# A graph layer on one core: gathers begun in fours at given counts of tiles

## The chip, the cores and the metric

One NeuronCore of a Trainium2 chip runs the whole kernel. The metric is the device time of one execution in microseconds, the median of several runs. Five engines work side by side, each through its own queue in order: TensorE (PE in the profile; PEld is its weight load), VectorE (DVE), ScalarE (ACT), GpSimd (POOL) and SyncE (SP). They wait for one another by semaphores.

## The reference

A layer of a graph network with 12,500 nodes and 400,000 edges, 64 features, edges sorted by their destination:

```python
h = feat_src @ node_w.T
rf = review_feat @ review_w.T
m = (h[src_idx] + rf) * edge_w
x = _layernorm(x + segment_sum(m, dst_idx, num_segments=12500))
```

For each edge the row of its source node and the edge's own attributes are multiplied by two 64x64 matrices, added, weighted and summed into the row of the destination node; the result is added to x and normalized over the features.

## The kernel before

Both products are linear, so the kernel sums first and multiplies once at the end: `sums` holds, for each node, 64 weighted sums of source rows and 64 of edge attributes. Edges come in tiles of 128, and the tiles are worked in two ways that share the engines.

**Units.** The first 116 x 2048 edges form 116 units of 16 tiles. SyncE loads a unit's attributes (L410), GpSimd gathers the rows of x for each of its 16 tiles by an indirect DMA, 128 rows of 256 bytes (L490), into one of four slots of `rows`. TensorE then sums the unit (`sum_unit`, L1156, instructions on L1166) with 32 matmuls, waiting for the attributes, for all 16 gathers (L1161) and for the buffer. ScalarE copies the result, TensorE brings it into a window of 128 nodes (`multiply_unit`, L1177) and VectorE adds the window to `sums`. Sums of a unit raise `unit_summed`, which frees its slot: the gathers of unit u wait for the sums of unit u - 4 (L485). Four units make a batch, whose indices are prepared together (`src_ready`).

**Counted tiles.** The other 1269 tiles (`COUNTED`) need no gather. For each tile VectorE makes two one-hot matrices (`hot_key` L746, `hot_lo` L747), TensorE multiplies them into a table of counts (six matmuls, L1235, raising `counted` once a tile) and ScalarE copies the table out (L1048). They go in 71 groups: group 0 has `GT0` = 9 tiles, each other one `GT` = 18. After a group's tiles TensorE multiplies the table with the whole of x (`sum_x`, L1260, 196 instructions); half way through, it turns the next group's indices (L1212 to L1216) and sometimes a batch's (L1150 to L1153).

**The order of the work** is written out by hand, and the same on all engines. Groups 1 to 70 are steps of seven rounds of ten; a step takes `STEPS` = 2, 1, 2, 1, 2, 2, 1, 2, 1, 2 units along. The first unit of a step is summed ahead of the group's tiles, the second, if there is one, after six of them. So ten groups take 16 units and 180 tiles. Six rounds are a hardware loop, the last is written out. After the groups the last four units (112 to 115) are summed in the tail, behind the multiplication of most nodes' sums (L1289).

**GpSimd's queue** holds, after some constants, the gathers of all units in order, and at the end the scaling of some blocks of the output (L575). In the loop a unit's bounds of waits depend on the round, so they are computed in registers. `gathers_begun` is raised once a unit; nothing waits for it.

Of the kernel before, what the change touches and what calls it, by code (L numbers as in the profile page):

```python
# [43 lines left out]
GT = 18  # L44
HOT_BUFS = 3
SPAN = 7
UT = 16
SLOTS = 4
BATCH = 4
CYCLE = 16  # L50
UNITS = 116
STEPS = (2, 1, 2, 1, 2, 2, 1, 2, 1, 2)
LATE_UNITS = 4
PAD = 32
BEGUN = 2
FAR = -1000.0
LN_EPS = 1e-5
# [2 lines left out]
def build(nc, x, src, dst, attr, weight, node_w, review_w, out):  # L60
# [7 lines left out]
    COUNTED = (EDGES - COUNTED_FROM) // P  # L68
    GROUPS = (COUNTED - 1) // GT + 1
    GT0 = COUNTED - (GROUPS - 1) * GT  # L70
# [2 lines left out]
    HI = (NODES - 1) // P + 1  # L73
    HALF = HI * SPAN // 2
    ROUND_GROUPS = len(STEPS)
    ROUNDS = (GROUPS - 1) // ROUND_GROUPS - 1
    BT = BATCH * UT
    BATCHES = UNITS // BATCH
    QUADS = P // PAD
    BLOCKS_U = UT // QUADS  # L80

    assert EDGES == ALL_CHUNKS * CHUNK and 2 * F == P
    assert sum(STEPS) == CYCLE and CYCLE == 4 * BATCH and SLOTS == BATCH and UNITS % BATCH == 0
    assert GROUPS - 1 == (ROUNDS + 1) * ROUND_GROUPS and UNITS == (ROUNDS + 1) * CYCLE + LATE_UNITS
    assert GT0 >= HOT_BUFS and GT % HOT_BUFS == 0 and UNITS <= P and GROUPS <= P
# [22 lines left out]
    with ExitStack() as ctx:  # L108
        def sb(name, shape, dt=F32):
            return ctx.enter_context(nc.sbuf_tensor(name, shape, dt))  # L110
# [24 lines left out]
        slot_dst = sb("slot_dst", [P, BATCH, BATCH * BLOCKS_U])  # L135
        unit_hot = [sb(f"unit_hot{b}", [P, UT, PAD]) for b in range(2)]
        slot_hot = [sb(f"slot_hot{b}", [P, BLOCKS_U, WIN]) for b in range(2)]
# [44 lines left out]
        at, g_dst = part(0, GROUPS, [GT, P], I32)  # L182
        at, g_lo_hi = part(at, GROUPS, [2, GT])
        at, g_wide = part(at, GROUPS, [2, GT])
        at, g_bad = part(at, GROUPS, [1, 8])
        at, u_dst = part(at, UNITS, [UT, P], I32)
        at, u_lo_hi = part(at, UNITS, [2, UT])
        at, u_wide = part(at, UNITS, [2, UT])
        at, u_bad = part(at, UNITS, [1, 8])
        at, u_last = part(at, UNITS, [1, 1])  # L190
        at, slot_far = part(at, NS, [2, GT])
        at, bad_row = part(at, 1, [1, GROUPS + UNITS])
        at, u_rows = part(at, 1, [2, UNITS])
        at, g_worst = part(at, 1, [1, 2])
        at, calm = part(at, 1, [4, LATE_UNITS])
# [4 lines left out]
        at, dst_i = part(0, ALL_CHUNKS, [1, CHUNK], I32)  # L200
        at, ones = part(at, P, [1, P])
        at, lo_diag = part(at, ALL_CHUNKS, [1, ALL_CHUNKS])
        at, lo_hi_col = part(at, ALL_CHUNKS, [1, 2])
        at, lo_hi_row = part(at, 1, [2, ALL_CHUNKS])
        at, windows_i = part(at, 1, [2, ALL_CHUNKS], I32)
        at, windows_f = part(at, 1, [2, ALL_CHUNKS])
        at, lo_all = part(at, P, [1, ALL_CHUNKS])
        at, base_tab = part(at, 1, [1, ALL_CHUNKS], I32)
        at, window_tab = part(at, 1, [1, ALL_CHUNKS + 1], I32)
        at, src_sb = part(at, P, [CHUNK_SLOTS, TILES], I32)  # L210
        at, dst_sb = part(at, P, [CHUNK_SLOTS, TILES], I32)
        at, w_sb = part(at, P, [CHUNK_SLOTS, TILES])
        at, dst_left = part(at, P, [1, TILES])
        at, scatter = part(at, P, [PART_BUFS, PER_PART * WIN])
# [47 lines left out]
        gathers_begun = sem("gathers_begun")  # L262
# [30 lines left out]
        counted = sem("counted")  # L293
# [62 lines left out]
        def round_steps(r):  # L356

            i, adds = 0, r * (CYCLE + ROUND_GROUPS) + 1
            for n, size in enumerate(STEPS):
# [3 lines left out]
                if isinstance(r, int) and batch and batch.q >= BATCHES:  # L363
                    batch = None
                yield Step(r * ROUND_GROUPS + n + 1, units, batch, adds)
                i += size
                adds += size + 1

        last_units = [unit_at(ROUNDS + 1, i) for i in range(LATE_UNITS)]
        last_adds = (ROUNDS + 1) * (CYCLE + ROUND_GROUPS) + 1  # L370

        def each_unit(eng, do):

            with eng.Fori(0, ROUNDS + 1) as r:
                for i in range(CYCLE):
# [17 lines left out]
        def _(sp):  # L393
# [11 lines left out]
            def load_attr(unit):  # L405

                s = unit.i % SLOTS
                if not isinstance(unit.u, int) or unit.u >= SLOTS:
                    sp.wait_ge(unit_summed, unit.u - SLOTS + 1 + BEGUN)
                sp.dma_start(rows[:, s, :, F:2 * F],  # L410
# [38 lines left out]
            with sp.If(is_narrow(sp) == 1):  # L449
                for i in range(SLOTS, CYCLE):  # L450
                    load_unit(unit_at(0, i))
                with sp.Fori(1, ROUNDS + 1) as r:
                    for i in range(CYCLE):
# [23 lines left out]

        @block.gpsimd
        def _(pool):
            def gather_unit(unit):  # L480

                s, c = unit.i % SLOTS, unit.i // BATCH
                pool.wait_ge(src_ready, unit.b + 1)
                if not isinstance(unit.u, int) or unit.u >= SLOTS:
                    pool.wait_ge(unit_summed, unit.u - SLOTS + 1 + BEGUN)  # L485

                pool.sem_inc(gathers_begun, 1)
                for t in range(UT):
                    k = unit.i % BATCH * UT + t
                    pool.indirect_dma_start(  # L490
                        out=rows[:, s, t, 0:F], out_offset=None, in_=x,
                        in_offset=bass.IndirectOffsetOnAxis(ap=src_cols[:, c, k:k + 1].bitcast(U32), axis=0),
                    ).then_inc(gathered[s], 16)

            def gather_chunk(c, s, r):
# [5 lines left out]
                for k in range(TILES):  # L501
# [7 lines left out]
            pool.memset(first_mask[:, 1, :], 0.0).then_inc(masks_made, 1)  # L509
            pool.iota(quad_of[:, :], pattern=[[1, QUADS], [0, PAD]], base=0, channel_multiplier=0,  # L510
                      allow_small_or_imprecise_dtypes=True).then_inc(masks_made, 1)
# [67 lines left out]
        def _(dve):  # L579
# [27 lines left out]
            def make_unit_hot(unit):  # L607

                h, k = unit.i % 2, unit.i % BATCH * UT
                dve.wait_ge(batch_read, unit.b + 1)  # L610
                dve.wait_ge(unit_summed, unit.u - 1 + BEGUN)
                hot = unit_hot[h][:, :, 0:SPAN]
# [7 lines left out]
            def make_slot_hot(unit):  # L620

                k = unit.i % BATCH * BLOCKS_U
                dve.wait_ge(batch_read, unit.b + 1)
                dve.wait_ge(unit_multiplied, unit.u - 1 + BEGUN)
                dve.tensor_tensor(slot_hot[unit.i % 2][:, :, :],  # L625
# [4 lines left out]
            def copy_unit(unit):  # L630

                dve.wait_ge(unit_summed, unit.u + 1 + BEGUN)
                dve.tensor_copy(unit_slots[unit.i % 2][:, :], unit_ps[:, :]).then_inc(unit_copied, 1)

            def add_unit(unit, before):

                base = dve.value_load(unit_tab[0:1, bass.ds(unit.u, 1)], min_val=0, max_val=NODES - 1)
                dve.wait_ge(added, before)
                dve.wait_ge(unit_multiplied, unit.u + 1 + BEGUN)
                dve.tensor_tensor(sums[:, bass.ds(base, WIN)], sums[:, bass.ds(base, WIN)], unit_window_ps, ALU.add  # L640
# [192 lines left out]
            dve.memset(all_ones[:, :], 1.0)  # L833
            step(dve.tensor_scalar(part_i[:, 1:2], part_i[:, 0:1], PAD - 1, None, ALU.bitwise_and))
            step(dve.tensor_copy(part_f[:, 1:2], part_i[:, 1:2]))
# [306 lines left out]
        def _(pe):  # L1142
# [13 lines left out]
            def sum_unit(unit):  # L1156
# [6 lines left out]
                for b in range(BLOCKS_U):  # L1163
                    for j in range(QUADS):
                        t = b * QUADS + j
                        done = pe.matmul(unit_ps[j * PAD:(j + 1) * PAD, b * 2 * F:(b + 1) * 2 * F],  # L1166
                                         unit_hot[h][:, t, :], rows[:, s, t, :], start=True, stop=True)
# [223 lines left out]
```

## Time and profile before

| what | us |
|---|---|
| median of three timed runs | 2600.75 |
| lowest and highest of them | 2598.28, 2603.38 |
| span of the profiled execution | 4402.7 |
| TensorE matmuls busy in it | 2973.6 (68%) |
| VectorE | 1620.1 (37%) |
| ScalarE | 1200.5 (27%) |
| GpSimd | 1855.3 (42%) |

The profiled execution took 4402.7 us, and the shares are of that span; the timed runs are 1802 us shorter. All durations of single instructions below come from the profiled execution. In the rows of the trace an instruction stands with its start, its duration, its engine and its line; in square brackets is the idle time of its engine before it, and what ended it. "remote" is a semaphore whose rise came late or whose sender the trace doesn't tell. In the chain of waits every piece is what the end was waiting for at that time; "issue" there is time in which the engine waited for nothing that the profile shows.

### The profile page before, as it was taken

What the parts mean: (1) busy time and instruction counts of PE and PEld (TensorE: products, weight loads), DVE (VectorE), ACT (ScalarE), POOL (GpSimd) and SP (SyncE); (2) the same over time, 40 slices, a digit from 0 to 9 for tenths busy, and PEclk for the clock granted to TensorE, in tenths of its full rate; (3) what the DMA queues carried; (4) which work ended last, traced back from release to release, by engine and by line L of the source; (5) the groups of instructions that cost most, each with busy time, mean ns of one, the idle gap of its engine ahead of it and who ended that gap; (6) DMA issues with size and microseconds to landing.
All of it is one profiled execution on the core that took longest, in us unless ns stands there. A gap on an engine that the chain in (4) does not pass through costs nothing.

```text
span 4402.7 us, 74924 instructions
## 1 busy us (share of the span) xinstructions
PE 2973.6 (68%) x28844; PEld 2163.7 (49%) x28845; DVE 1620.1 (37%) x4276; ACT 1200.5 (27%) x1951; POOL 1855.3 (42%) x1885
## 2 busy tenths in 40 slices
PE   1767776776766766757777767777567567677676
PEld 1445553555544545535555545455345445455555
DVE  3333332343333333324333333333234333333334
ACT  0222222332222222213222222223223222222223
POOL 5444335434344443453344444443443344444342
PEclk9777787887777787778787777788778777777787
DMA  4121111111111121111111111211111122122111
GB/s 88 41 42 41 40 40 40 40 41 41 41 36 39 39 42 38 40 41 39 40 41 38 40 37 40 42 42 39 39 42 38 35 42 42 36 42 47 34 40 42
DMA packets 491784, 181.43 MB, mean 41 GB/s; under 512 B 449029, under 2 KB 461508, under 8 KB 491206
## 3 DMA queue, kind: packets, MB, share of 16 engines
q1 hardware_dynamic: 259490, 68.52, 7.2%
q0 software_dynamic: 59392, 60.94, 7.2%
q10 hardware_dynamic: 172510, 46.74, 4.9%
q8 instruction: 247, 4.05, 0.4%
q14 instruction: 145, 1.19, 0.1%
HBM read 172.85 MB, written 3.20 MB: 40 GB/s over the span
## 4 chain that ended last, share of the span: by engine, by line
PE 57%; another core or an unknown queue 27%; issue 10%; ACT 4%; DVE 1%; ACTq 1%; DVEq 0%; DMA 0%; SPq 0%; POOL 0%; POOLq 0%
PE count_ps L1235 30%; PE x_sums_ps L1260 18%; ACT counts L1048 4%; PE unit_ps L1166 3%; PE attr_ps L1227 2%; PE turn_ps L1177 1%; PE x_sums_ps L1268 1%; PE turn_ps L1215 1%; DVE hot_lo L747 0%; PE turn_ps L1212 0%; ACTq L1081 0%; PE x_sums_ps L1269 0%; PE attr_ps L1150 0%; DVE hot_key L746 0%
## 5 line engine op out<-in xcount | busy, mean ns | idle before, releaser
L490 POOL DMA_INDIRECT rows<-x,src_cols x1856 | 1845.6, 994 | 2475.0 <-PE unit_ps L1166 1434.0
L1235 PE MATMUL count_ps<-hot_key,hot_lo 128*128 128x343 bf16 x7614 | 1627.5, 366 | 1066.7 <-ACT counts L1048 613.5
L1235 PEld LDWEIGHTS count_ps<-hot_key,hot_lo 128*128 128x128 bf16 x7614 | 799.2, 115 | 1683.7 <-issue 842.1
L1048 ACT ACTIVATE counts<-count_ps 128x686 f32<-128x686 f32 x1269 | 1009.0, 803 | 1752.6 <-remote 947.4
L746 DVE TENSOR_SCALAR hot_key<-count,cols 128x686 bf16<-128x686 f16 x1269 | 531.5, 419 | 2128.6 <-remote 1185.3
L1260 PE MATMUL x_sums_ps<-counts,x_tab 128*64 128x126 f32 (+1 forms) x13916 | 804.6, 275 | 55.9 <-ACT counts L1048 54.8
L1260 PEld LDWEIGHTS x_sums_ps<-counts,x_tab 128*64 128x64 f32 x13916 | 771.2, 139 | 73.3 <-ACT counts L1048 68.8
L747 DVE SCALAR_TENSOR_TENSOR hot_lo<-count,cols 128x384 bf16<-128x384 f16 x1269 | 776.5, 612 | 0.0
L1166 PE MATMUL unit_ps<-rows,unit_hot 128*32 128x128 f32 x3712 | 223.1, 289 | 182.1 <-issue 176.2
L1227 PEld LDWEIGHTS attr_ps<-hot_rel,g_attr 128*128 128x128 f32 x1270 | 257.7, 230 | 94.9 <-issue 59.9
L1166 PEld LDWEIGHTS unit_ps<-rows,unit_hot 128*32 128x32 f32 x3712 | 123.3, 112 | 259.1 <-issue 252.5
L1227 PE MATMUL attr_ps<-hot_rel,g_attr 128*128 128x14 f32 x1270 | 222.2, 248 | 38.8 <-issue 31.1
L1021 ACT ACTIVATE unit_slots<-unit_ps 128x512 f32<-128x512 f32 x112 | 66.9, 598 | 530.6 <-remote 400.2
L1177 PE MATMUL turn_ps<-slot_hot,unit_slots 128*128 128x128 f32 x928 | 130.1, 286 | 0.6 <-DVE sums L640 0.6
L1177 PEld LDWEIGHTS turn_ps<-slot_hot,unit_slots 128*128 128x128 f32 x928 | 125.1, 203 | 7.9 <-issue 1.6
L1066 ACT ACTIVATE x_sums<-x_sums_ps 128x126 f32<-128x126 f32 (+1 forms) x71 | 19.6, 276 | 368.6 <-PE x_sums_ps L1260 368.6
L761 DVE TENSOR_TENSOR hot_rel<-column,cols 128x126 f32<-128x126 f32 (+1 forms) x71 | 20.6, 291 | 230.9 <-ACT cols L1032 230.9
L1030 ACT ACTIVATE slot_rel<-turn_ps,slot_no 126x1 f32<-126x1 f32 (+1 forms) x71 | 18.5, 261 | 318.4 <-PE turn_ps L1216 271.5
L782 DVE TENSOR_TENSOR sums<-sums,turn_ps 128x128 f32 x71 | 20.5, 289 | 199.1 <-PE turn_ps L1276 184.0
L625 DVE TENSOR_TENSOR slot_hot<-column,slot_dst 128x512 f32<-128x512 f32 x116 | 79.7, 687 | 2.6 <-issue 2.6
L605 DVE CAST src_cols<-attr_ps 128x64 int32<-128x64 f32 x29 | 6.5, 225 | 141.3 <-ACT rel_cols L1014 141.3
L1013 ACT ACTIVATE slot_dst<-attr_ps,part_f 128x16 f32<-128x16 f32 x29 | 7.9, 274 | 175.1 <-PE attr_ps L1153 175.1
(136 smaller groups left out, 953.1 us busy)
## 6 DMA issues: line engine op xcount, KB each, us to landing
rows<-edge_attr SPq DMA_DIRECT2D x116, 512.0 KB
g_attr<-edge_attr ACTq DMA_DIRECT2D x70, 576.0 KB, 4.6
rows<-x,src_cols POOLq DMA_INDIRECT x1856
out<-x_tab SPq DMA_DIRECT2D x10, 256.0 KB
g_idx<-src ACTq DMA_DIRECT2D x70, 9.0 KB
g_idx<-dst ACTq DMA_DIRECT2D x70, 9.0 KB
g_w<-edge_weight ACTq DMA_DIRECT2D x70, 9.0 KB
stage<-src SPq DMA_DIRECT2D x29, 32.0 KB
```

The lines of the kernel that those rows point to most:

```text
L490: pool.indirect_dma_start(out=rows[:, s, t, 0:F], out_offset=None, in_=x, in_offset=bass.IndirectOffsetOnAxis(ap=src_cols[:, c, k:k + 1].b ...
L625: dve.tensor_tensor(slot_hot[unit.i % 2][:, :, :], column[:, :].unsqueeze(1).to_broadcast([P, BLOCKS_U, WIN]), slot_dst[:, unit.i // BATCH ...
L746: dve.tensor_scalar(hot_key[h][:, :], count16[:, :], cols[:, KEY, t:t + 1], None, ALU.is_equal)
L747: made = dve.scalar_tensor_tensor(hot_lo[h][:, :, :], count16[:, 0:P].unsqueeze(1).to_broadcast([P, 3, P]), cols[:, LO, t:t + 1], cols[:, ...
L1021: act.activation(unit_slots[unit.i % 2][:, :], unit_ps[:, :], ACT.Copy).then_inc(unit_copied, 1)
L1048: act.activation(counts[:, :, t * SPAN:(t + 1) * SPAN].rearrange("p (a h) d -> p a h d", a=2), count_ps[t % 2][:, :, 0:HALF].rearrange("p ...
L1166: done = pe.matmul(unit_ps[j * PAD:(j + 1) * PAD, b * 2 * F:(b + 1) * 2 * F], unit_hot[h][:, t, :], rows[:, s, t, :], start=True, stop=True)
L1177: done = pe.matmul(unit_window_ps, unit_slots[unit.i % 2][:, b * 2 * F:(b + 1) * 2 * F], slot_hot[unit.i % 2][:, b, :], start=(b == 0), st ...
L1215: pe.transpose(turn_ps[:, q * GT:q * GT + nt], packed[0:nt, q, :], ident[0:nt, 0:nt])
L1227: pe.matmul(attr_ps[0:(until - t) * F, t * SPAN:until * SPAN], g_attr[:, t:until, :].rearrange("p t f -> p (t f)"), hot_rel[:, t:until, :] ...
L1235: last = pe.matmul(count_ps[b][:, a, 0:HALF], hot_lo[h][:, i, :], hot_key[h][:, a * HALF:(a + 1) * HALF], start=(i == 0), stop=(i == 2))
L1260: done = pe.matmul(x_sums_ps[half * F:(half + 1) * F, 0:ns], x_tab[:, hi, :], counts[:, hi, 0:ns], start=(hi < 2), stop=(hi >= HI - 2))
```

## The change

From unit 4 on, GpSimd waits ahead of each four of a unit's 16 gathers until TensorE has counted a given number of tiles, and then raises `gathers_begun` once more. 64 gathers of a batch are spread over `BATCH_TILES` = 10 x 18 x 4 / 16 = 45 tiles; the count is that of an even spread, less `LEAD` = 28 tiles. For the k-th gather of batch b it is 45 b + 9 + (45 k / 64, rounded down) - 28. Where it is known at build time it is cut to `COUNTED`. The waits of a unit ahead of its first gather stay.

```diff
@@ -52,6 +52,8 @@
 STEPS = (2, 1, 2, 1, 2, 2, 1, 2, 1, 2)
 LATE_UNITS = 4
 PAD = 32
+BURST = 4
+LEAD = 28
 BEGUN = 2
 FAR = -1000.0
 LN_EPS = 1e-5
@@ -73,6 +75,7 @@
     HI = (NODES - 1) // P + 1
     HALF = HI * SPAN // 2
     ROUND_GROUPS = len(STEPS)
+    BATCH_TILES = ROUND_GROUPS * GT * BATCH // CYCLE
     ROUNDS = (GROUPS - 1) // ROUND_GROUPS - 1
     BT = BATCH * UT
     BATCHES = UNITS // BATCH
@@ -477,6 +480,12 @@
 
         @block.gpsimd
         def _(pool):
+            def tiles_counted(unit, t):
+
+                at = GT0 + (unit.i % BATCH * UT + t) * BATCH_TILES // BT - LEAD
+                after = unit.b * BATCH_TILES + at
+                return min(after, COUNTED) if isinstance(after, int) else after
+
             def gather_unit(unit):
 
                 s, c = unit.i % SLOTS, unit.i // BATCH
@@ -486,6 +495,11 @@
 
                 pool.sem_inc(gathers_begun, 1)
                 for t in range(UT):
+                    if t % BURST == 0 and (not isinstance(unit.u, int) or unit.u >= SLOTS):
+                        after = tiles_counted(unit, t)
+                        if not isinstance(after, int) or after > 0:
+                            pool.wait_ge(counted, after)
+                            pool.sem_inc(gathers_begun, 1)
                     k = unit.i % BATCH * UT + t
                     pool.indirect_dma_start(
                         out=rows[:, s, t, 0:F], out_offset=None, in_=x,
```

## Rows read from the trace of the kernel before

**Rows 1.** The first line of the page of the kernel before.
```profile
span 4402.7 us, 74924 instructions
```

**Rows 2.** Three stretches, all engines: us, then busy us (instructions), granted clock, DMA share.
```profile
4341.94:4402.73 60.79, 35.72 (x362) 33.34 (x362) 33.21 (x75) 25.94 (x86) 5.87 (x7) 0.82 0.22 54
0.00:117.80 117.80, 27.79 (x301) 19.30 (x302) 46.44 (x123) 10.32 (x21) 65.03 (x86) 1.00 0.45 88
117.80:4341.94 4224.14, 2910.11 (x28181) 2111.11 (x28181) 1540.42 (x4079) 1164.29 (x1844) 1784.35 (x1792) 0.78 0.19 40
```

**Rows 3.** Who waited for whom, groups 1 to 70: us in total, times, longest.
```profile
POOL rows L490 <- PE unit_ps L1166: 1434.0, 64, 32.9
DVE hot_key L746 <- remote: 1161.7, 207, 23.8
```

**Rows 4.** Chain of waits without gathers: start us, us, what, instructions.
```profile
2038.26 0.13 PE attr_ps L1227 x2
...
2040.29 0.13 PE attr_ps L1227 x2
...
2042.35 0.81 ACT counts L1048
...
2043.21 5.59 PE x_sums_ps L1260 x98
...
2055.01 1.01 PE unit_ps L1166 x32
...
2056.60 0.18 PE attr_ps L1227 x2
```

**Rows 5.** Chain of waits around the group before, partly beside gathers.
```profile
1999.90 0.32 PE attr_ps L1150 x2
...
2000.67 0.30 PE turn_ps L1212 x2
...
2014.49 0.89 PE turn_ps L1177 x8
...
2019.59 4.43 issue
```

**Rows 6.** GpSimd in order of time: the first and the 64th gather.
```profile
9.82 1.15 POOL L490 DMA_INDIRECT rows<-x,src_cols  x1 [4.82 <-DVE src_cols L605]
...
89.29 0.95 POOL L490 DMA_INDIRECT rows<-x,src_cols  x1 [0.30 <-issue]
```

**Rows 7.** GpSimd, first and last of seven gathers beside counting.
```profile
2008.73 0.95 POOL L490 DMA_INDIRECT rows<-x,src_cols  x1 [29.32 <-PE unit_ps L1166]
...
2016.78 0.95 POOL L490 DMA_INDIRECT rows<-x,src_cols  x1 [0.30 <-issue]
```

**Rows 8.** GpSimd, last gather of unit 100 and first of unit 101.
```profile
3772.89 0.95 POOL L490 DMA_INDIRECT rows<-x,src_cols  x1 [0.30 <-issue]
3774.14 1.19 POOL L490 DMA_INDIRECT rows<-x,src_cols  x1 [0.30 <-issue]
```

**Rows 9.** TensorE in order of time: the unit's sums that free a slot.
```profile
2006.82 1.08 PE L1166 MATMUL unit_ps<-rows,unit_hot 128*32 128x128 f32 x32
```

**Rows 10.** All engines in order of time, the tail.
```profile
4328.84 13.06 PE L1260 MATMUL x_sums_ps<-counts,x_tab 128*64 128x126 f32 x196 [1.19 <-ACT counts L1048]
...
4368.28 1.05 POOL L575 TENSOR_TENSOR x_tab<-x_tab,counts 128x512 f32<-128x512 f32 x1 [42.70 <-DVE counts L822]
...
4373.30 13.22 ACT L1136 ACTIVATE x_tab<-x_tab,counts 128x64 f32<-128x64 f32 x55
...
4380.14 1.08 PE L1166 MATMUL unit_ps<-rows,unit_hot 128*32 128x128 f32 x32
```

**Rows 11.** Who waited for whom in the head, 50 to 117.8 us.
```profile
DVE hot_key L746 <- remote: 23.6, 2, 15.4
```

**Rows 12.** Two lines of the kernel: ns min/median/max, first and last start.
```profile
L490 POOL DMA_INDIRECT rows<-x,src_cols x1856: 942/947/1390, 9.8 to 4324.6; - x186
...
L485 POOLq ALU_OP  x84: 32/32/49, 614.7 to 4127.1; - x84
```

## The prediction

> **What bounds the kernel now.** The first thing to read is the distance between the two times: the profiled execution spans 4402.7 us [rows 1], the timed runs 2600.75 us. Nothing that is only said of the profiled execution may be sold as a gain, so I read the profile by stages to see which part of it the timed runs can contain.
>
> The stretches [rows 2] are the head up to the sums of group 0 (117.8 us), 70 groups (4224.1 us) and the tail (60.8 us). In the groups TensorE is granted 0.78 on average, a mix of its two levels (2.4 and 1.2 GHz), against 1.00, the full 2.4 GHz, in the head. The waits of that stretch [rows 3] name GpSimd waiting for a slot (1434 us, 64 times), and VectorE waiting for a semaphore that came late (1161.7 us). In the chain of waits the late semaphores are visible: while gathers are issued, one tile is followed by 4.43 us in which TensorE waits [rows 5]; once the gathers of a unit are out, two tiles take 2040.29 - 2038.26 = 2.03 us [rows 4].
>
> Now add up a group from its undisturbed pieces. From the end of one group's x sums to the first tile 2056.60 - 2055.01 = 1.59 us (one unit's sums, 1.01, are in it); 18 tiles at 1.015 = 18.27; the last copy 0.86; the x sums with the turning of the next group's rows 2055.01 - 2043.21 = 11.80 [rows 4]. Ten groups hold 16 units: 1.6 window products at 0.89 = 1.42 [rows 5], 0.6 further unit sums at 1.01 = 0.61, and 0.4 turnings of a batch at 2000.67 - 1999.90 = 0.77, that is 0.31 [rows 5]. Sum: 34.86 us a group, 2440 us for 70. With head and tail as profiled that makes 2440 + 117.8 + 60.8 = 2619; the head itself holds late semaphores (VectorE alone lost 23.6 us to them [rows 11]), and without those it is 2595. The timed 2600.75 lies between. So the 4224 - 2440 = 1784 us that the groups lose beside gathers are in the profiled execution alone; in the timed runs TensorE's own chain of count, x sums and unit sums accounts for everything but a few us. TensorE bounds the kernel, in every group.
>
> Second is GpSimd. The first 64 gathers, with VectorE nearly idle, begin (89.29 - 9.82)/63 = 1.26 us apart [rows 6]; seven beside full counting begin (2016.78 - 2008.73)/6 = 1.34 us apart [rows 7]. A group needs 256/10 = 25.6 gathers. Of a group's 34.86 us, 20.3 are counting and 14.6 not: 14.6/1.26 = 11.6 gathers in the latter, 14.0 at 1.34 = 18.8 us in the former, 33.4 us together. GpSimd is busy 96% of the timed run, and has 1.5 us to spare a group. From above: a single gather took up to 1390 ns [rows 12], with the 0.30 us before it [rows 7] 1.69; but the timed run itself excludes such a mean, since the last unit is summed 4380.14 - 4341.9 = 38.2 us into the tail [rows 10]: 1856 gathers fit into 2600.75 - 60.8 + 38.2 - 9.8 = 2568 us, so their mean is at most 1.384. I take 1.30, and keep 1.26 to 1.384.
>
> **The change part by part.** Nothing is removed; every unit still waits for its slot. Added is, from unit 4 on, a wait for a count of tiles ahead of each four gathers, with a semaphore increment: 112 x 4 = 448 gates, 6.4 a group. Queued behind a gate on GpSimd are the later gathers and, at the end, its scalings; who waits for them is TensorE at a unit's sums (L1161) and SyncE's last stores. SyncE's loads of edge attributes and everything else of the five queues stay where they were.
>
> Cost of a gate that is already open: the same pair, a wait and an increment, stands at each unit's beginning now. Between two units inside the loop whose slot was free, the gathers begin 3774.14 - 3772.89 = 1.25 us apart [rows 8], as within a unit. So 0 us: the sequencer handles it while earlier gathers run. The loop also computes each bound: its register operation takes 32 ns [rows 12], hidden likewise; if nothing hid it, 2 x 0.03 x 6.4 = 0.4 us a group, within the spare 1.5.
>
> Cost of a gate that is shut: TensorE ends a unit's sums at 2006.82 + 1.08 = 2007.90, the gather begins at 2008.73 [rows 9, 7], 0.83 us later, against 0.30 between gathers: 0.53 us lost, plus the idle time itself. How often? Gates open with tiles, 2.8 tiles apart. In counting that is 2.9 us, while four gathers take 5.2: GpSimd falls behind and finds the gates open. In the x sums no gate opens, and it works off what is left: 33.4 us of gathers become due in about 20 us, leaving some 13 us for the 14.6 us without counting. So about one shut gate a group: 33.4 + 0.5 = 33.9 of 34.86. It still fits, by 0.9 us.
>
> Does TensorE ever wait for a gather? By the constants, unit u's first gate is at 45(u/4) - 19 + 11.25(u%4) tiles (u/4 whole) and its last burst some 8 tiles on. Against the counts at which the steps sum units (two-unit groups at 0 and 6 tiles, others at 0), the last gate leads by 15 tiles at least (unit 9 of a round: 90 against 105), 25 at most. Before, a unit could begin as soon as the unit four before it was summed, 36 to 48 tiles ahead. So the lead shrinks, but 15 tiles span a group's end here: 15 x 1.015 + 0.86 + 11.80 + 1.59 = 29 us, more than the 13 us of backlog and a burst of 5.2. No wait; 0 us.
>
> Head: unit 4 begins at tile 26 instead of tile 9, some 19 us later, out of GpSimd's spare and wanted at tile 51: 0 us.
>
> Tail: the last bounds would lie beyond the 1269 counted tiles and are cut to that. From the last group's start 12 bursts (units 113 to 115) become due: 48 gathers, about 15 at 1.34 and 33 at 1.26 = 62 us, begun some 2 us after counting starts. That counting takes 18.27 + 2 x 0.89 + 1.01 = 21 us and the rest to the end of the x sums 12.7, so the gathers end about 64 - 34 = 30 us into the tail. Unit 115 is summed at 38.2 us: hidden by 8 us, without the landing. GpSimd's first scaling, at 4368.28 - 4341.9 = 26.4 us now, moves back some 4 us; ScalarE's scalings, whose blocks are stored first, run to 4373.30 + 13.22 = 4386.5, 44.6 us in [rows 10], and hide it. 0 us.
>
> Sum: 0 us against the profiled execution's undisturbed chain, so 2601 us.
>
> A rule that speaks against the change is weighed by itself. Beside counting a gather step takes 1.34 us instead of 1.26 [rows 6, 7]. The Trainium skill (SBUF — State Buffer, "Who interferes with whom") says that a VectorE instruction in a two-port mode and GpSimd shut each other out of the port they share, so that descriptors from GpSimd wait until it ends; it quotes 620 ns growing to 3100. By such a factor gathers let go only by counted tiles would bound the kernel; the trace shows 6%, and this rule is part of the third case below.
>
> **The rivals.**
> Faster: some of the timed run's few us of stalls beside gathers go, because bursts are spread. For it: the 4.43 us waits exist in the profiled execution. Against: the sum leaves room for 2601 - 2595 = 6 us; if the head holds another dozen us of late semaphores, about 18. And GpSimd stays 96% busy, so there is little to spread. 2583 to 2595, say 2592.
> The change does nothing: the gates are always open when GpSimd reaches them. Then 2601 too; it belongs to the forecast.
> Slower, GpSimd becomes the bound: it decides where a group's gathers and gates pass 34.86 us, that is at 0.14 us for each gate (0.9/6.4), or a mean gather of 1.34. If every gate cost what a shut one does, 33.4 + 6.4 x 0.53 = 36.8 a group, 1.9 x 70 = 136 us, less the lead of about 20: 2717. If gathers are at their upper bound 1.384, 35.4 + 0.5 = 35.9, 1.1 x 70 - 20 = 55 us: 2656. Half of that is likelier: 2630. For it: 96%. Against: the free boundary of rows 8.
> Slower, the tail: the last gathers come later than 38 us, because late semaphores or VectorE's closing work stretch them; 8 us are covered, 15% more on 62 us is not: 2607.
>
> **How the numbers follow.** Hidden, with the change that does nothing: 0.55, 2601. Faster: 0.20, 2592. GpSimd bound: 0.20, 2607 to 2717. Tail: 0.05, 2607. About 0.2% (5 us) is what a measurement of this kernel can tell from no change; so faster 0.20, same 0.55, slower 0.25. The range takes in the lower end of the faster case, 2584, and above it the bound case up to its second price, rounded to 2650; outside lie about 0.03 below and 0.08 above.
>
> **What would show it.** In the changed profile GpSimd's long waits for unit sums (64, 1434 us) should be replaced by many shorter ones released by the tiles' matmuls; 1856 gathers at 1.26 to 1.34 still; no extra gap where a burst begins behind an open gate; two undisturbed tiles still 2.03 us and x sums 11.80; the last gather some 30 us into the tail instead of ahead of it. The profiled span may move by hundreds of us either way, since its stalls hang on how gathers bunch; that says nothing of the timed runs. The prediction is wrong if TensorE waits at L1161 for gathers, if steps at the burst's boundary exceed 1.4 us with the gate open, or if the timed run moves while these rows don't.

## The result and the profile after

| | us |
|---|---|
| kernel before, median | 2600.71 (2597.80 to 2603.38) |
| changed kernel, median | 2604.56 (2601.12 to 2608.32) |
| ratio, 95% interval | 1.0015 [1.0008, 1.0021] |
| span of the profiled execution of the changed kernel | 2603.8 |
| span of the kernel before, profiled once more, unchanged | 2597.0 |

The change makes the kernel 3.9 us longer (0.0015 x 2600.7; 2.1 to 5.5 by the interval). That is less than the 0.2% named as the bound of a difference, and still not nothing. The span of [rows 1], 4402.7 us, was that one execution: the same program, profiled again, spans 2597.0 us. So the trace after is laid beside this second trace of before.

In what follows the head ends with the first group's x sums, and the tail begins with the end of the last group's x sums. The three stretches (columns as in [rows 2]: us, busy us and instructions of TensorE, its weight loads, VectorE, ScalarE, GpSimd, then the granted clock, the DMA share and GB/s), first of the changed kernel:

```profile
0.00:80.73 80.73, 25.34 (x301) 18.87 (x302) 46.69 (x122) 10.45 (x21) 57.95 (x78) 1.00 0.64 124
80.73:2540.55 2459.82, 2395.24 (x28182) 1902.58 (x28181) 1533.86 (x4079) 1176.68 (x1844) 1824.91 (x1777) 0.99 0.33 68
2540.55:2603.80 63.25, 38.96 (x363) 36.33 (x362) 35.11 (x75) 25.93 (x86) 29.89 (x32) 0.79 0.28 65
```

and of the kernel before, profiled again:

```profile
0.00:74.54 74.54, 24.64 (x301) 18.62 (x302) 45.09 (x120) 10.44 (x21) 52.81 (x73) 1.00 0.67 132
74.54:2534.95 2460.41, 2393.73 (x28181) 1901.17 (x28181) 1538.57 (x4083) 1176.18 (x1844) 1846.07 (x1798) 1.00 0.34 68
2534.95:2597.00 62.05, 36.74 (x362) 34.34 (x362) 33.24 (x75) 25.91 (x86) 13.14 (x15) 0.80 0.24 58
```

The 70 groups take the same time, 2459.8 and 2460.4 us, with TensorE's clock at its full level (0.99 and 1.00 of 2.4 GHz). In the tail GpSimd is busy 29.89 us instead of 13.14, and the tail is 1.2 us longer. That alone says little: the unchanged kernel's own two profiles differ as much in it (60.8 us in [rows 2], 62.0 here). The head is 6.2 us longer, which the experiments have to judge.

Who waits for whom in the groups, from 82 to 2530 us (us in total, times, longest), of the changed kernel:

```profile
POOL rows L504 <- PE count_ps L1249: 160.6, 233, 12.5
...
PE x_sums_ps L1274 <- ACT counts L1062: 46.8, 70, 0.7
...
PE unit_ps L1180 <- issue: 14.4, 5, 3.1
```

GpSimd's waits for unit sums are gone; it waits for tiles instead. TensorE has no wait for a gather. Its five waits at the unit sums L1180, 14.4 us in all, stand in the unchanged kernel too (14.4 us, 5 times), at the turns of the loop.

The gates, in GpSimd's order of time: an open one, and a shut one with the last gather ahead of it.

```profile
1506.32 0.95 POOL L504 DMA_INDIRECT rows<-x,src_cols  x1 [0.30 <-PE count_ps L1249]
...
1528.47 1.97 POOL L504 DMA_INDIRECT rows<-x,src_cols  x1 [0.30 <-issue]
1534.08 0.98 POOL L504 DMA_INDIRECT rows<-x,src_cols  x1 [3.63 <-PE count_ps L1249]
```

An open gate leaves the 0.30 us that stands between any two gathers [rows 7, 8]. The shut one was let go by a tile of the group that TensorE began at 1532.22 us, behind x sums and a unit's sums.

The tail, in order of time. First the changed kernel, from its last gather on:

```profile
2571.03 0.95 POOL L504 DMA_INDIRECT rows<-x,src_cols  x1 [0.30 <-issue]
...
2572.00 4.82 POOL L589 TENSOR_TENSOR x_tab<-x_tab,counts 128x512 f32<-128x512 f32 x5
...
2572.90 0.65 DVE L647 COPY unit_slots<-unit_ps 128x512 f32<-128x512 f32 x1
2573.47 2.77 DVE L629 TENSOR_TENSOR unit_hot<-column,rel_cols 128x112 f32<-128x112 f32 x1
...
2581.42 1.08 PE L1180 MATMUL unit_ps<-rows,unit_hot 128*32 128x128 f32 x32
```

then the kernel before, profiled again:

```profile
2562.51 1.04 POOL L575 TENSOR_TENSOR x_tab<-x_tab,counts 128x512 f32<-128x512 f32 x1 [18.15 <-DVE counts L822]
...
2567.48 1.76 POOL L575 TENSOR_TENSOR x_tab<-x_tab,counts 128x512 f32<-128x512 f32 x2 [0.17 <-DVE counts L822]
...
2568.33 0.33 DVE L615 TENSOR_TENSOR unit_hot<-column,rel_cols 128x112 f32<-128x112 f32 x1
...
2574.31 1.08 PE L1166 MATMUL unit_ps<-rows,unit_hot 128*32 128x128 f32 x32
```

Before, GpSimd's five scalings are begun one by one, as VectorE makes their factors, and are nearly done when VectorE makes the one-hot matrices of unit 114 (L615, after the change L629). After, the last gather ends at 2571.98, 31.4 us into the tail; by then the factors are ready, and five scalings run one behind the other through the moment in which VectorE wants to make them. Its instruction takes 2.77 us instead of 0.33. In the chain of waits it now has a piece of its own, as no such instruction has in the unchanged kernel's chain:

```profile
2572.90 0.65 DVE unit_slots L647
2573.55 2.70 DVE unit_hot L629
...
2577.71 1.93 PE unit_ps L1180 x32
2579.64 1.85 PE turn_ps L1191 x8
2581.49 1.01 PE unit_ps L1180 x32
```

Unit 115 is summed 2581.42 - 2540.55 = 40.9 us into the tail; in the unchanged kernel 2574.31 - 2534.95 = 39.4. The same part of the unchanged kernel's chain:

```profile
2568.55 1.70 PE unit_ps L1166 x32
2570.25 2.01 PE turn_ps L1177 x8
2572.26 1.03 PE unit_ps L1166 x32
2573.29 1.09 PE turn_ps L1177 x8
2574.38 1.01 PE unit_ps L1166 x32
```

This pair alone doesn't show that the collision costs the 1.5 us. Unit 114's sums begin 37.2 us into the tail in both (2577.71 and 2572.19). What differs behind that is the clock granted to TensorE: its lower level (0.50 of 2.4 GHz) covers 2574.4 to 2581.1 us in the changed kernel, with unit 114's sums and the window product behind them in it (1.93 and 1.85 us), and 2568.9 to 2572.2 in the unchanged one, where the same two come after it (1.03 and 1.09 us). To see what the collision costs takes more executions; they stand side by side below.

### The profile page after: what moved, and what is told of

It is laid out like the page before. It is cut to its first block, busy times and chain, and to the rows that moved or that the text cites. A ratio compares the mean times of both kernels' runs of the same rounds, so it can differ in the third digit from the quotient of the medians.

```text
span 2603.8 us, 75732 instructions
## 1 busy us (share of the span) xinstructions
PE 2459.5 (94%) x28844; PEld 1957.8 (75%) x28845; DVE 1615.7 (62%) x4276; ACT 1213.1 (47%) x1951; POOL 1912.8 (73%) x1885
## 4 chain that ended last, share of the span: by engine, by line
PE 93%; ACT 2%; DVE 2%; issue 1%; DMA 1%; SPq 0%; DVEq 0%; POOL 0%; POOLq 0%; ACTq 0%
PE count_ps L1249 46%; PE x_sums_ps L1274 30%; PE unit_ps L1180 5%; PE turn_ps L1191 4%; PE attr_ps L1241 4%; ACT counts L1062 2%; PE x_sums_ps L1282 1%; PE turn_ps L1229 1%; PE turn_ps L1226 1%; DMA counts<-dst 1%; PE x_sums_ps L1283 1%; DVE sums L902 0%; PE count_ps L1303 0%; PE attr_ps L1164 0%; DVE x_tab L825 0%
## 5 line engine op out<-in xcount | busy, mean ns | idle before, releaser
L504 POOL DMA_INDIRECT rows<-x,src_cols x1856 | 1903.1, 1025 | 663.8 <-issue 498.5
L1249 PE MATMUL count_ps<-hot_key,hot_lo 128*128 128x343 bf16 x7614 | 1277.9, 312 | 0.0
L1062 ACT ACTIVATE counts<-count_ps 128x686 f32<-128x686 f32 x1269 | 1019.4, 803 | 382.0 <-PE count_ps L1249 360.1
L1249 PEld LDWEIGHTS count_ps<-hot_key,hot_lo 128*128 128x128 bf16 x7614 | 697.1, 101 | 397.0 <-issue 119.1
L1274 PE MATMUL x_sums_ps<-counts,x_tab 128*64 128x126 f32 (+1 forms) x13916 | 788.5, 271 | 48.7 <-ACT counts L1062 47.8
L1274 PEld LDWEIGHTS x_sums_ps<-counts,x_tab 128*64 128x64 f32 x13916 | 755.0, 137 | 64.5 <-ACT counts L1062 60.1
L1241 PEld LDWEIGHTS attr_ps<-hot_rel,g_attr 128*128 128x128 f32 x1270 | 210.1, 192 | 36.3 <-issue 14.1
L1241 PE MATMUL attr_ps<-hot_rel,g_attr 128*128 128x14 f32 x1270 | 193.8, 227 | 5.0 <-issue 3.1
L1044 ACT ACTIVATE slot_rel<-turn_ps,slot_no 126x1 f32<-126x1 f32 (+1 forms) x71 | 18.5, 261 | 294.0 <-PE turn_ps L1230 294.0
L1180 PE MATMUL unit_ps<-rows,unit_hot 128*32 128x128 f32 x3712 | 127.4, 278 | 19.8 <-issue 14.4
L1180 PEld LDWEIGHTS unit_ps<-rows,unit_hot 128*32 128x32 f32 x3712 | 95.7, 110 | 37.8 <-issue 31.5
```

The costliest lines, as they stand in the source:

```text
L504: pool.indirect_dma_start(out=rows[:, s, t, 0:F], out_offset=None, in_=x, in_offset=bass.IndirectOffsetOnAxis(ap=src_cols[:, c, k:k + 1].b ...
L1062: act.activation(counts[:, :, t * SPAN:(t + 1) * SPAN].rearrange("p (a h) d -> p a h d", a=2), count_ps[t % 2][:, :, 0:HALF].rearrange("p ...
L1241: pe.matmul(attr_ps[0:(until - t) * F, t * SPAN:until * SPAN], g_attr[:, t:until, :].rearrange("p t f -> p (t f)"), hot_rel[:, t:until, :] ...
L1249: last = pe.matmul(count_ps[b][:, a, 0:HALF], hot_lo[h][:, i, :], hot_key[h][:, a * HALF:(a + 1) * HALF], start=(i == 0), stop=(i == 2))
L1274: done = pe.matmul(x_sums_ps[half * F:(half + 1) * F, 0:ns], x_tab[:, hi, :], counts[:, hi, 0:ns], start=(hi < 2), stop=(hi >= HI - 2))
```

## The experiments

The theory (T): the cost is in the tail. The late gathers push GpSimd's scalings onto VectorE's one-hot instruction, and that delays units 114 and 115. The rivals: the gates themselves cost about 9 ns each (G, 3.9 us / 448), or the head is longer because units 4 and later are held back in it (H). Two further kernels measure how much room GpSimd and the lead have. "Into the tail" is counted from the end of the last x sums.

### The kernel before, once more

Nothing is edited; the question is whether 4402.7 us belongs to the order of the gathers.

> The kernel before, unchanged, profiled once more. If the stalls beside gathers belong to this kernel under the profiler (sixteen gathers in a row as soon as a slot is free), its span is near 4400 us again. If they belonged to that one execution, the span is near 2600 us, and the trace then shows the undisturbed kernel before, whose tail can be compared.

Span 2597.0 us, time 2598.7, groups 2460.4 instead of 4224.1 [rows 2]. The late semaphores of [rows 3] belong to one execution. What brought them in it isn't known.

### Gates everywhere but for the last four units

```diff
-if t % BURST == 0 and (not isinstance(unit.u, int) or unit.u >= SLOTS):
+if t % BURST == 0 and (not isinstance(unit.u, int) or SLOTS <= unit.u < UNITS - LATE_UNITS):
```

> The change with the gates of units 4 to 111 only; units 112 to 115 are begun as before, as soon as their slots are free. Theory T (the 3.9 us that the change costs lie in the tail, where GpSimd's last gathers end 31 us after the last x sums, so that its five scalings run back to back and hold up one VectorE instruction by 2.4 us): the last gather ends at most 27 us after the last x sums, that instruction takes 0.3 us again, and the time is that of before, 2600.7 us (ratio 1.000, within 0.0005). Rival G (the 448 gates cost something each, 3.9/448 = 9 ns): 432 of 448 are still there, so 2604.4 us (1.0014).

A miss. The tail was not relieved: the last gather still ends 31.4 us into it, the instruction takes 2.77 us, the tail 63.6. The gates of the units up to 111 alone have put GpSimd that far behind, so 48 gathers are still queued without any gate of their own. Ratio 1.0006 [0.9998, 1.0015], between nothing and the change. The run doesn't separate T from G.

### Gates for the last four units alone

```diff
-if t % BURST == 0 and (not isinstance(unit.u, int) or unit.u >= SLOTS):
+if t % BURST == 0 and isinstance(unit.u, int) and unit.u >= UNITS - LATE_UNITS:
```

> The kernel before with the gates of units 112 to 115 alone (16 gates). Theory T: 2604.5 us (1.0015), the last gather ends 30 us after the last x sums and the VectorE instruction that makes unit 114's one-hot matrix takes over 2 us. Rival G: 16 gates of 448, 2600.8 us (1.000).

Sixteen gates instead of 448. Last gather 31.5 us into the tail, the one-hot instruction 4.02 us, the tail 64.1 us. Ratio 1.0006 [0.9998, 1.0015], 1.6 us: the tail is as long as with all gates, the time lies lower than the change's, with an interval that overlaps the change's and holds 1. It speaks for T as to the tail and is too coarse as to the time.

### The lead cut from 28 tiles to 18

```diff
-LEAD = 28
+LEAD = 18
```

> The change with LEAD = 18 instead of 28: each gate opens ten tiles later. By the prediction's working the last gate of unit 9 of a round then leads its sums by 5 tiles only, all in counting: 29 us less 10 x 1.015 tiles and less the x sums when the gate falls behind them, against a burst of 5.3 us and what is queued. Theory L (the lead of 15 tiles is what keeps TensorE from waiting, and the change stands some 17 us above the point where it begins to): TensorE waits some 2 us at one or two unit sums of a round and some 15 us for the last unit in the tail, 2635 to 2650 us (1.013 to 1.019). Rival (GpSimd has room and the lead doesn't matter): 2604 to 2608 us.

2666.5 us, ratio 1.0250 [1.0235, 1.0265]. The waits in its groups now name the gathers' landing:

```profile
PE unit_ps L1180 <- DMA rows<-x,src_cols: 33.9, 13, 3.5
```

The direction is right, the size was underrated: groups 2510.5 us (50 longer, at two of the ten steps of a round, by 1.9 and 5.4 us), and tail 77.5 (14 longer), which the expectation had left out. The last gather ends 51.3 us into the tail and unit 115 is summed at 53.1. Ten tiles less lead use up the change's whole reserve.

### The lead raised from 28 tiles to 36

```diff
-LEAD = 28
+LEAD = 36
```

> The change with LEAD = 36 instead of 28: all 448 gates stay, each opens eight tiles earlier. The traces so far put the groups at 2460 us in the kernel before and with the change alike, and the tail 1.3 to 2.1 us longer with the change. Theory T (the cost is in the tail alone): the last gather ends 12 to 20 us into the tail, VectorE's instruction that took 2.77 us takes 0.3, the tail is 62 us again, the groups 2460, and the time is that of before, ratio 1.000 within the interval. Rival G (gates cost): the ratio stays at 1.0015. Smallest distance from a unit's last gather to its sums: about 30 us, against 17.8 with LEAD = 28.

The gates are the same in number; all are eight tiles earlier. The last gather ends 17.9 us into the tail, the one-hot instruction takes 0.33 us again, the tail 62.0. Ratio 1.0002 [0.9993, 1.0011], 2601.7 us. A cost of each gate would have kept the ratio at 1.0015, which the interval leaves out; G falls.

### The change, once more

> The change itself once more, beside the other three on one chip, with a second profile. Theory T: ratio 1.0006 to 1.0015, groups 2460 us, tail 63 to 64 us; the head, which differed by 6 us between profiled executions of kernels that are equal there, is anywhere between 74 and 81 us. Rival H (the change makes the head longer, 80.7 us in its first profile against 74.5): the head is near 80.7 us again.

Ratio 1.0015 [1.0006, 1.0024], as the first time. Tail 64.4 us; the collision is larger, 4.02 us:

```profile
2573.66 4.84 POOL L589 TENSOR_TENSOR x_tab<-x_tab,counts 128x512 f32<-128x512 f32 x5
2573.90 4.02 DVE L629 TENSOR_TENSOR unit_hot<-column,rel_cols 128x112 f32<-128x112 f32 x1
```

The head is 78.8 us, again longer than the 74.5 of before, which keeps H alive.

### A gate ahead of every gather

```diff
-BURST = 4
+BURST = 1
```

> The change with BURST = 1: a gate ahead of each gather, 1792 in place of 448, the last gate of a unit two tiles later than now. Theory T: open gates cost nothing, groups 2460 us, the tail as with the change, ratio 1.0006 to 1.0015. Rival G (each gate costs 9 ns or more): 1792 gates cost 15.6 us, 2616 us, ratio 1.006. Third case of the prediction (GpSimd becomes the bound because gates cost time on its queue): at 0.2 us a gate 1344 more gates are 269 us of GpSimd, ratio over 1.04.

Four times as many gates: 2604.6 us, ratio 1.0009 [1.0000, 1.0018], groups 2462.7 us. A cost of 9 ns a gate would have made 16 us; G falls a second time. The collision is there, at the one-hot instruction of the last unit: 2.52 us, last gather 32.9 us into the tail.

### A seventeenth gather in each unit

```diff
+pool.indirect_dma_start(out=spare_rows[:, s, :], out_offset=None, in_=x, in_offset=...).then_inc(gathered[s], 16)
...
-pe.wait_ge(gathered[s], (unit.b + 1) * (16 * UT))
+pe.wait_ge(gathered[s], (unit.b + 1) * (16 * (UT + 1)))
```

The kernel before, with its last gather of each unit made twice, the second into a buffer that nobody reads. It measures how near GpSimd is to being the bound.

> The kernel before with a 17th gather in each unit: the last tile's rows once more, into a buffer that nothing reads, and 17 x 16 instead of 16 x 16 awaited. 116 more gathers at 1.31 to 1.35 us are 152 to 157 us of GpSimd. By the prediction GpSimd is 96% busy, so it becomes the bound: 27.2 x 1.305 = 35.5 us a group at the least and 27.2 x 1.35 = 36.7 at the most, against 35.1 measured for a group, up to 110 us over the run less some 60 us of lead, and some 17 us for the last unit in the tail: 2613 to 2670 us (1.005 to 1.027). Rival (GpSimd has room to spare): 2601 to 2604 us.

2660.9 us, ratio 1.0229 [1.0213, 1.0244]. In the chain of waits GpSimd's gathers stand one behind the other, and TensorE waits for their landing:

```profile
PE unit_ps L1171 <- DMA spare_rows<-x,src_cols: 28.4, 5, 6.0
```

A gather step is 1.314 us here without the few that take longer, 1.332 with them; 27.2 of them a group are 35.74 to 36.2 us, against the 35.14 us that a group takes otherwise. Over 70 groups that is 42 to some 75 us; the groups are 2499.6 - 2460.4 = 39 us longer, because the lead is used up first: unit 57 is the first whose sums wait for its gathers. The tail is 18.5 us longer besides. So one gather in sixteen more, and GpSimd is the bound.

### Before, with the scalings held back

```diff
-pool.wait_ge(rstd_ready, ACT_BLOCKS + n + 1)
+pool.wait_ge(rstd_ready, max(ACT_BLOCKS + n + 1, len(early)))
```

> The kernel before with one wait changed: GpSimd begins its first five scalings only when the last of the early blocks has its factor, about 33 us into the tail instead of 26 to 28; no gate anywhere, gathers as before. Theory T (the scalings, pushed back by the late gathers, run at the moment VectorE makes the one-hot matrices of units 114 and 115): VectorE's instruction takes 2.5 to 4 us instead of 0.3, unit 115 is summed 40 to 41 us into the tail instead of 39.4, the tail is 63 to 64.5 us instead of 62.0, the time 1 to 2.5 us longer than before (ratio 1.0004 to 1.0010). Rival H (the cost of the change lies in the head, where the gates hold units 4 and later back): no difference here, ratio 0.9997 to 1.0003, tail 62.

The scalings run one behind the other, begun 32.6 us into the tail. But the collision is smaller than T said:

```profile
2571.64 4.83 POOL L575 TENSOR_TENSOR x_tab<-x_tab,counts 128x512 f32<-128x512 f32 x5 [23.17 <-DVE counts L822]
2572.03 0.78 DVE L615 TENSOR_TENSOR unit_hot<-column,rel_cols 128x112 f32<-128x112 f32 x1
2572.85 1.00 DVE L618 TENSOR_TENSOR unit_hot<-unit_hot,rel_cols 128x112 f32<-128x112 f32 x1
2574.87 1.02 DVE L615 TENSOR_TENSOR unit_hot<-column,rel_cols 128x112 f32<-128x112 f32 x1
```

Here VectorE gets through each time one scaling ends (2572.68, 2573.72 and 2575.75). With late gathers, it got through only after the fourth, at 2576.05 in the changed kernel. Unit 115 is summed at 39.6 us, the tail is 62.4, the ratio 0.9995 [0.9987, 1.0004]. A miss for T: back-to-back scalings alone don't cost what they do behind the late gathers.

### Gates in the first round alone

```diff
-if t % BURST == 0 and (not isinstance(unit.u, int) or unit.u >= SLOTS):
+if t % BURST == 0 and isinstance(unit.u, int) and SLOTS <= unit.u < CYCLE:
```

> The change with gates for units 4 to 15 alone (48 gates, the first round); from unit 16 on as before. Rival H: the profiled head is 78 to 81 us as in the two profiles of the change (80.7 and 78.8), not 74 to 76 as in the kernel before (74.5), and the time is 1.5 to 4 us over the kernel before (ratio 1.0006 to 1.0015). Theory T: head as it happens to fall, tail 62 us, one-hot instruction 0.3 us, ratio 0.9997 to 1.0004.

Head 78.4 us, as H had said, and yet 2601.9 us and ratio 0.9994 [0.9986, 1.0003]: H falls. The order of the gathers says the same. The first gate stands behind the 64th gather, and in the changed kernel that begins at 91.60 us, after the head's end at 80.73:

```profile
91.60 0.95 POOL L504 DMA_INDIRECT rows<-x,src_cols  x1 [0.30 <-issue]
103.47 0.94 POOL L504 DMA_INDIRECT rows<-x,src_cols  x1 [10.92 <-PE count_ps L1249]
```

The head's length differs from one profiled execution to the next without the gates: it is 77.7 us in the kernel above, which has none, and 80.7 and 73.6 in two executions of the next kernel, which has all. In part this is a load ahead of the first tile. From 0 to 82 us, first the unchanged kernel (head 74.5), then the changed one (80.7):

```profile
ACT x_tab L1078 <- DMA counts<-dst: 11.9, 1, 11.9
```

```profile
ACT x_tab L1092 <- DMA counts<-dst: 17.0, 1, 17.0
```

These are 5.1 of the 6.2 us. In the present run that wait is 12.6 us, only 0.7 longer, with a head 3.9 us longer; what else stretches the head is open.

### The change, with the scalings behind the one-hot matrices

```diff
 for unit in last_units:
     gather_unit(unit)
+pool.wait_ge(unit_hot_made, 2 * UNITS)
```

All gates and all late gathers remain; GpSimd only begins its scalings when VectorE has made the matrices of unit 115.

> The change with one wait added: GpSimd begins its scalings only when VectorE has made the one-hot matrices of unit 115, some 2 us later than in the changed kernel. Theory T: no one-hot instruction of the tail takes over 0.4 us, unit 115 is summed at about 39.4 us, the tail is 61.5 to 62.5 us, the time 1 to 2.5 us under the changed kernel's: 2602 to 2604 where the kernel before takes 2601 (ratio 1.0002 to 1.0010). Rival H: the time stays where the changed kernel's was, ratio 1.0012 to 1.0018, even if the tail is shorter in the profile. Should the late stores of GpSimd's blocks set the end instead, the tail is longer than 63 us though the instruction is short.

The rows that stood at 2.77 and 4.82 us:

```profile
2574.59 0.27 DVE L630 TENSOR_TENSOR unit_hot<-column,rel_cols 128x112 f32<-128x112 f32 x1
...
2577.31 0.27 DVE L630 TENSOR_TENSOR unit_hot<-column,rel_cols 128x112 f32<-128x112 f32 x1
...
2578.16 5.63 POOL L590 TENSOR_TENSOR x_tab<-x_tab,counts 128x512 f32<-128x512 f32 x5 [3.83 <-DVE unit_hot L633]
```

Unit 115 is summed at 37.8 us, the tail is 60.4 us; 2602.5 us, ratio 0.9997 [0.9989, 1.0006]. Unit 115, the tail and the ratio lie below what T had said, on the side away from H. The kernel before was some 2 us slower beside it than beside the change, so it was measured again:

> The change with GpSimd's scalings held until VectorE has made the last one-hot matrices, once more: in the first comparison the ratio was 0.9997 [0.9989, 1.0006], but the kernel before was slower there (2603.2) than beside the two runs of the change (2600.7, 2601.6). Theory T (the collision in the tail is the cost): ratio 0.9995 to 1.0007, median under 2603.5, no one-hot instruction of the tail over 0.4 us, tail 60 to 62 us. Rival G (448 gates cost 9 ns each, the tail nothing): ratio 1.0011 to 1.0019, median 2604 to 2606. Between them, 1.0007 to 1.0011, the tail carries about half.

2600.7 us, ratio 0.9996 [0.9987, 1.0005], tail 61.5, last gather 31.5 us into it, no one-hot instruction of the last units over 0.28 us. Both intervals end below 1.0008, where the change's begins (1.0006 the second time). With the collision taken away and everything else of the change left in, the cost is gone. This kernel may win back a little that the change didn't cost: in the unchanged kernel too, unit 114's two one-hot instructions are longer beside the last scalings, 0.33 and 0.68 us instead of the 0.27 and 0.28 here.

### The tails side by side

| kernel | last gather, us into the tail | unit 112's sums begin, us into the tail | longest first one-hot instruction (L629 in the changed kernel) of units 113 to 115 | tail | ratio |
|---|---|---|---|---|---|
| before, again | 9.4 | 27.7 | 0.33 | 62.0 | 1 |
| change | 31.4 | 27.6 | 2.77 | 63.3 | 1.0015 |
| change, again | 31.5 | 26.5 | 4.02 | 64.4 | 1.0015 |
| not the last units | 31.4 | 27.6 | 2.77 | 63.6 | 1.0006 |
| last units alone | 31.5 | 26.4 | 4.02 | 64.1 | 1.0006 |
| a gate for every gather | 32.9 | 26.5 | 2.52 | 62.4 | 1.0009 |
| lead 36 | 17.9 | 26.5 | 0.33 | 62.0 | 1.0002 |
| first round alone | 9.5 | 26.5 | 0.33 | 60.1 | 0.9994 |
| scalings held back, no gates | 9.4 | 27.8 | 1.02 | 62.4 | 0.9995 |
| scalings behind the matrices | 31.5 | 26.5 | 0.27 | 60.4 | 0.9997 |
| the same, again | 31.5 | 26.5 | 0.27 | 61.5 | 0.9996 |

The five executions with an instruction over 2.5 us have a mean tail of 63.6 us and a mean ratio of 1.0010. The five with 0.27 to 0.33 us, the kernel before among them, have a mean tail of 61.2; the four ratios among these average 0.9997. That is 2.4 us of tail and 3.4 us of time (0.0013 x 2601); a tail is that of one execution, a time that of eleven to twenty, and the 1 us between them isn't located.

The clock is a rival for the tails, which differ by a microsecond with it. The kernel with the scalings behind the matrices has no collision in either execution; unit 114's sums take 1.08 us in one and 1.94, at the lower level, in the other, and the tails are 60.4 and 61.5. And where unit 112's sums begin at 27.6 to 27.8 us instead of 26.5, TensorE was longer at its lower level early in the tail (from 3.2 to 10.0 us into it in the kernel before, against 4.4 to 7.8 in the change, again). So compare tails that begin alike. Among those with 26.4 or 26.5, the three with a collision have a mean of 63.6 and the four without one 61.0; at 27.6 and 27.7, the change has 63.3 and the gates without the last units 63.6, and the kernel before 62.0. A difference of 1.3 to 2.6 us remains. How much of it comes by way of the lower level that follows a collision, as in the first pair above, isn't shown.

No kernel with a short instruction is slower than 1.0002. No version was measurably faster than the kernel before.

## Why the prediction was right, and where it was not

*What bounds the kernel.* Right. The sum was 34.86 us a group and 2595 to 2619 in all, with the stalls of [rows 2, 3] left out as belonging to one execution; the groups of the second profile of before take 2460.4 / 70 = 35.15 us, 20 us more over the 70. A piece that the sum didn't have accounts for more than that: at the turn of the loop a group takes 41.3 to 42.5 us, where the round that is written out has 36.0 at the same place, five times in a run, 30 us in all. That 2595 came so near to the timed run was luck: its head of 94 us measured 74.5, and these 20 us too many stood against the groups' 20 too few.

*The gates.* Right. An open gate costs nothing (row 1506.32 above; 1792 gates leave the time where 448 put it). Shut gates were forecast at about one a group; 45 of the 448 show a step over 1.7 us, 0.6 a group. They cost GpSimd idle time only: 160.6 us in the groups, less 233 x 0.30 that any step has, is 91 us, where it lost 62 us to unit sums before (76.3 us in 46 waits there).

*GpSimd's reserve.* Right, and as narrow as forecast. Steps under 1.7 us average 1.318 us where 1.30 was taken; with the 29 gathers that take about 1.9 us each, the steps without a wait average 1.33. 25.6 of them are 33.7 to 34.1 us of a group's 35.14, so 1.0 to 1.4 us are spare where the sum had 0.9 after its shut gates. The extra gather shows the third case's mechanism at its price: 6% more work on GpSimd costs 2.3%. The gates don't bring it about, since they are open or cost idle time that it has. The 6% that the prediction set against the rule on two-port modes doesn't test that rule: no row tells in which mode VectorE's instructions ran.

*The lead.* Right. TensorE never waits for a gather in the changed kernel. The sum left 29 - 13 - 5.2, about 11 us, between a unit's last gather and its sums; the shortest distance in the groups is 17.8 us (the median 27.6, and 53.5 in the kernel before), so the mechanism held and the size was too low. With lead 18 the reserve is used up.

*The head.* Right, 0 us (first round alone: 0.9994).

*The tail.* This is the step that failed: the term of 0 us measured 2.4 us in the tails and 3.4 to 3.9 us in the times. Its first half held: the last gathers end 31.4 us into the tail (forecast: 30), and unit 115 would have been summed in time. Its second half said that GpSimd's scalings move back and ScalarE's longer scalings hide it. The scalings did move by 4 us (from 27.6 to 31.5 us into the tail), and the stores behind them were hidden: begun even later, behind the matrices, they leave a tail of 60.4. But they also kept VectorE from its own instruction, which took 2.5 to 4.0 us instead of 0.3, and [rows 10] showed when the first one stood (4368.28) without the prediction asking what runs on VectorE at the time to which it moves. The fourth case, a slower tail at 2607 with a chance of 0.05, has the right place and nearly the right size, and the wrong mechanism: it asked for gathers later than 38 us.

*The faster case.* Nothing of it: the groups are equal within 0.6 us. Its "few us of stalls beside gathers" were in the first profile of before alone.

So 2601 against 2604.6 was close, in the class of no difference, because three large terms were rightly found hidden; the small difference that is left comes from the one term that was costed by its own engine alone.

## What to carry to other kernels

A step that is moved must be costed at the place where it lands: ask which instructions of every other engine run there, not only who waits for the step. A gate on an engine with little reserve cost nothing here as long as the work queued behind it was done before its use; measure the reserve by adding one unit of work, as the seventeenth gather did. And where the profiled execution is far from the timed runs, add up the undisturbed pieces, and profile the same program once more: here the second profile showed that the difference belonged to the first execution.

## What the runs showed of the hardware

- VectorE's one-hot instruction with two inputs (column and rel_cols, 128x112) takes 0.27 us alone, 0.33 us beside the end of GpSimd's scalings, and 0.78 to 4.02 us in the midst of them. A copy of 128x512 from the matmul's buffer, in the same stretch, keeps its 0.65 us (row 2572.90). The Trainium skill (SBUF — State Buffer, "Who interferes with whom") says that a VectorE instruction with two SBUF inputs contends with a GpSimd instruction that reads SBUF, and that the one issued first keeps the shared ports for the whole instruction. The held-back scalings agree: VectorE gets through when one scaling ends. The changed kernel doesn't: it got through only after the fourth of five, in each of the runs with late gathers that collided. Why it was passed over between the scalings there is open; it wasn't tried apart.
- The same program spanned 4402.7 us in one profiled execution and 2597.0 in another.
- Where TensorE waits for a gather (lead 18, seventeenth gather), its sums begin about 1.7 us after the end of GpSimd's gather instruction, which is about when its rows have landed.
- In the tails of the table the granted clock is 0.77 to 0.82 on average, where TensorE waits again and again for VectorE's and ScalarE's closing work (busy 36.74 of 62.05 us in the unchanged kernel); the sums of a unit that take 1.08 us in the groups take up to 1.94 there, at the lower of the two levels.
